# Decoder layer with cross attention: end of the program interleaved, first steps rearranged, cross product in high and low parts

## What is computed

```python
x = layernorm(x + attn(x))      # 4 layers: local and linear attention, then a gelu MLP 256-1024-256
x = layernorm(x + xattn(x, ctx) @ Wout + bout)
x = layernorm(x + gelu(x @ W1c) @ W2c)
# xattn: query i sees only key j with j % n_q == i, n_q = 256, 120 keys
mask = j_idx % n_q == i_idx
sim = where(mask, q @ k.T * scale, -max)
out = softmax(sim) @ v
# W1c, W2c: top 32 of 64 primitives by logits, w = softmax(top values)
W1c = einsum('k,kir,kro->io', w, A[idx], B[idx])
```

## Time and profile before

| what | value |
|---|---|
| median of 3 runs | 1010.5 us (1009.2 to 1010.58) |
| profiled execution | 1011.33 us, span 1009.5 us |
| PE, DVE, ACT, POOL busy | 96%, 67%, 56%, 47% |
| chain that ended last | PE 86%, DVE 5%, SP's queue 2%, issue 2% |
| first two steps | 0 to about 98 us |
| context stage and hand-over | 724 to 782 us |
| compose W1, cross product, compose W2 | to 830, to 845, to 904 us |
| last stage | 904 to 1009.5 us |

### The profile page before, as it was taken

One profiled execution on the slowest core, in us unless ns is written; L12 is line 12 of the kernel. 1 busy time (PEld: TensorE's weight loads), 2 busy tenths in 40 slices (PEclk: granted clock), 3 DMA queues, 4 the chain that ended last, 5 costly groups with the idle time before them and its releaser, 6 DMA issues.

```text
span 1009.5 us, 21836 instructions
## 1 busy us (share of the span) xinstructions
PE 966.8 (96%) x8589; PEld 830.4 (82%) x8589; DVE 681.3 (67%) x1457; ACT 568.0 (56%) x1350; POOL 470.5 (47%) x368
## 2 busy tenths in 40 slices
PE   5869999999999999999999999999999989999997
PEld 4658888888888888888888888888888769998887
DVE  6686768677677868676776768676531886767543
ACT  3666666675856666575766766585623443454210
POOL 3346175456826563774547276551426230007441
PEclk9869999999999999999999999999999999999999
DMA  6030000001110000021000002010155793740001
GB/s 200 6 122 1 2 16 2 1 17 51 36 43 17 2 1 17 4 82 43 17 1 1 18 1 85 1 39 11 38 106 138 158 197 82 163 78 1 21 22 43
DMA packets 71549, 47.57 MB, mean 47 GB/s; under 512 B 44479, under 2 KB 68127, under 8 KB 71455
## 3 DMA queue, kind: packets, MB, share of 16 engines
q1 hardware_dynamic: 71455, 46.27, 18.1%
HBM read 44.16 MB, written 2.10 MB: 46 GB/s over the span
## 4 chain that ended last, share of the span: by engine, by line
PE 86%; DVE 5%; SPq 2%; issue 2%; ACT 2%; POOL 2%; DMA 1%; DVEq 0%; POOLq 0%; ACTq 0%
PE F L1446 19%; PE F L1293 18%; PE A L1293 14%; PE A L1602 4%; PE A L1391 4%; PE A L1749 4%; PE A L1349 3%; PE F L1306 3%; PE A L1408 2%; PE A L1306 2%; PE F L1286 2%; PE A L1722 1%; PE A L1286 1%; PE A L1382 1%; PE A L1365 1%
## 5 line engine op out<-in xcount | busy, mean ns | idle before, releaser
L1293 PE MATMUL F<-xt,w 128*128 128x512 f32 x864 | 218.6, 401 | 4.6 <-ACT scratch L1277 3.9
L431 POOL TENSOR_TENSOR ht<-scratch,ht 128x512 fp32r<-128x512 f32 x128 | 175.6, 1391 | 42.5 <-ACT ht L1081 41.0
L1293 PEld LDWEIGHTS F<-xt,w 128*128 128x128 f32 x864 | 157.5, 188 | 45.9 <-ACT scratch L1277 7.6
L1446 PE MATMUL F<-w,ht 128*128 128x256 f32 x1536 | 190.6, 283 | 2.0 <-POOL ht L431 2.0
L1446 PEld LDWEIGHTS F<-w,ht 128*128 128x128 f32 x1536 | 184.0, 189 | 7.8 <-issue 4.6
L419 POOL TENSOR_TENSOR rstd<-var,minus_half 128x4 f32<-128x4 f32 x32 | 37.6, 1174 | 192.1 <-DVE var L552 191.5
L1078 ACT ACTIVATE scratch<-F,b_now 128x512 f32<-128x512 f32 x128 | 87.5, 684 | 36.3 <-POOL ht L431 18.1
L1293 PE MATMUL A<-wa,xt 128*128 128x512 f32 x372 | 89.9, 397 | 0.0
L1081 ACT ACTIVATE ht<-scratch 128x512 fp32r<-128x512 f32 x128 | 81.0, 632 | 4.1
L1293 PEld LDWEIGHTS A<-wa,xt 128*128 128x128 f32 x372 | 69.3, 189 | 16.0 <-issue 0.2
L426 POOL TENSOR_TENSOR x<-x,vec_f 128x1024 f32<-128x1024 f32 x16 | 37.9, 2368 | 94.2 <-DVE scratch L572 94.2
(11 more groups left out here) (224 smaller groups left out, 2012.1 us busy)
## 6 DMA issues: line engine op xcount, KB each, us to landing
raw_f<-in_L_attn_W_dram SPq DMA_DIRECT2D x8, 1024.0 KB, 5.6
scratch<-in_L_ffn_fc_B_dram SPq DMA_DIRECT2D x32, 256.0 KB, 4.6
scratch<-in_L_ffn_fc_A_dram SPq DMA_DIRECT2D x32, 256.0 KB, 3.9
raw_f<-in_L_ffn_fc_A_dram SPq DMA_DIRECT2D x32, 64.0 KB, 3.9
scratch<-in_x_dram SPq DMA_DIRECT2D x1, 2048.0 KB, 12.4
raw_f<-in_L_ffn_fc_B_dram SPq DMA_DIRECT2D x32, 64.0 KB, 3.5
x<-in_x_dram SPq DMA_DIRECT2D x3, 512.0 KB, 6.7
out_dram<-x SPq DMA_DIRECT2D x3, 512.0 KB, 2.9
```

The source lines that it names most:

```text
L431: pool.tensor_tensor(ht[:, 1, m, :], hf[:, m % 2, :], ht[:, 0, m, :].bitcast(F32), ALU.subtract).then_inc(h_lo, 1)
L1293: last = pe.matmul(out, lhs(a, c), rhs(b, c), start=k == 0, stop=k == len(total) - 1)
L1446: last = pe.matmul(F[:, t % 2, 0:D], ht[:, a, c, P * t:P * t + P], w2[:, b, c, :], start=k == 0, stop=k == len(passes) - 1)
```

## The change

Five parts. (1) GpSimd's order in the first steps: one bias addition ahead of the W1 subtractions, the other behind the first `vec_f` bias, W2's subtractions at the end of the second step; `top_weigh` scales `chosen` (64x32) instead of a block of ones (64x128). (2) VectorE clamps the indices as it writes them, and SyncE's loads skip the runtime range check. (3) The context and `Wv Wout` are split in high and low parts (`ctx_rows`, `wvo_part`), the eight mean rows are one product (`mean_row`, `pick` selects the row), and the cross product runs on FP32R parts. (4) `pairs_lo` splits statistics and scaling in halves, VectorE's loop is written out, and pair 1 is multiplied ahead of the last item's output tiles. (5) In the last stage two gelu chunks and one output tile of the item before alternate, W2's parts are emptied between gelu chunks, and the last item is normalised and stored tile by tile. Scheduling changes that are not in the cut below: a wait of SyncE on `wvo_psum` is gone (the wait behind it covers it), and semaphores have new names.

```diff
+        ctx_rows = [[flat.rearrange("p (b t) -> p b t", b=B) for flat in parts] for parts in (
+            (wa_flat[:, 0:1024], wa_flat[:, 1024:2048]), (wa_flat[:, 2048:3072], wo_flat[:, 0:1024]))]
+        wvo_part = [[ht_odd[:, i, D * c:D * c + D] for c in range(DC)] for i in range(2)]
+        mean_row = [xt[1][:, i, 0, 0:D] for i in range(2)]
+        pick = xt[1][:, 0, 1, 0:P]
...
-                    index[0:1, bass.ds(first, 8)], engines=[mybir.EngineType.SP], min_val=0, max_val=PRIMS - 1)
+                    index[0:1, bass.ds(first, 8)], engines=[mybir.EngineType.SP], min_val=0, max_val=PRIMS - 1,
+                    skip_runtime_bounds_check_because="VectorE holds every index between 0 and PRIMS - 1 as it writes them")
...
+            pool_bias(pool, 0, 0, 0)
             split_lo(pool, w1_pieces(), w1_hi, w1_ready, 0)
-            pool_bias(pool, 0, 0, 0)
-            pool_bias(pool, 0, 1, 1)
...
-                if not out:
-                    split_w2_lo(pool, 0)
...
+                if not out:
+                    pool_bias(pool, 0, 1, 1)
...
+                if not out:
+                    split_w2_lo(pool, 0)
...
                 dve.reciprocal(lsum[:, :], A[0:PRIMS, 0, 0:2]).then_inc(top_step, 1)
-                dve.tensor_copy(index[:, :], A[0:1, 0, 64:64 + 2 * TOPK]).then_inc(index_ready, 1)
+                dve.tensor_scalar(index[:, :], A[0:1, 0, 64:64 + 2 * TOPK], 0.0, float(PRIMS - 1), ALU.max,
...
-                    last = dve.tensor_scalar(lw_wide[:, f, :], ones64[:, :], lw[:, f:f + 1], None, ALU.mult)
+                    last = dve.tensor_scalar(weighted[:, f, :], chosen[:, f, :], lw[:, f:f + 1], None, ALU.mult)
...
-                dve.wait_ge(wvo_psum, 2)
+                for c in range(DC):
+                    dve.wait_ge(cross_hi, c + 1)
+                    lo(dve, wvo_part[1][c], A[:, 4 + c, 0:D], wvo_part[0][c]).then_inc(cross_lo, 1)
                 for c in range(DC):
                     for s in range(2):
-                        dve.wait_ge(ctxt_psum, 2 * c + s + 1)
-                        dve.tensor_copy(ctxt[:, c, 4 * s:4 * s + 4, 0:NKV],
-                                        A[:, 2 * c + s, :].rearrange("p (b t) -> p b t", b=4)[:, :, 0:NKV]).then_inc(ctxt_out, 1)
-                dve.wait_ge(ctxt_out, 4)
-                dve.tensor_reduce(ctx_mean[:, :, :], ctxt[:, :, :, 0:NKV], AX_X, ALU.add).then_inc(ctx_sum, 1)
-                dve.wait_ge(ctx_sum, 1)
+                        rows = A[:, 2 * c + s, :].rearrange("p (b t) -> p b t", b=4)[:, :, 0:NKV]
+                        part = [ctx_rows[i][c][:, 4 * s:4 * s + 4, 0:NKV] for i in range(2)]
+                        dve.wait_ge(cross_hi, 2 + 2 * c + s + 1)
+                        lo(dve, part[1], rows, part[0]).then_inc(cross_lo, 1)
+                        dve.tensor_reduce(ctx_mean[:, c, 4 * s:4 * s + 4], rows, AX_X, ALU.add).then_inc(ctx_sum, 1)
+                dve.wait_ge(ctx_sum, 4)
+                dve.tensor_scalar(ctx_mean[:, :, :], ctx_mean[:, :, :], 1.0 / NKV, None, ALU.mult).then_inc(ctx_sum, 1)
+                dve.wait_ge(ctx_sum, 5)
                 for c in range(DC):
-                    last = dve.tensor_scalar(ctxt[:, c, :, NKV:CB],
-                                             ctx_mean[:, c, :].rearrange("p (b o) -> p b o", o=1).broadcast_to([P, B, CB - NKV]),
-                                             1.0 / NKV, None, ALU.mult)
-                last.then_inc(ctxt_ready, 1)
+                    part = [ctx_rows[i][c][:, :, NKV:CB] for i in range(2)]
+                    dve.wait_ge(cross_hi, 6 + c + 1)
+                    lo(dve, part[1], ctx_mean[:, c, :].rearrange("p (b o) -> p b o", o=1).broadcast_to([P, B, CB - NKV]),
+                       part[0]).then_inc(cross_lo, 1)
...
+            def mean_rows():
+                dve.wait_ge(h_psum, FC * ITEMS * DEPTH)
+                for i in range(2):
+                    dve.memset(mean_row[i].bitcast(F32), 0.0).then_inc(mean_zero, 1)
+            def mean_rows_lo():
+                dve.wait_ge(mean_zero, 2)
+                dve.wait_ge(mean_row_hi, 2)
+                lo(dve, mean_row[1][0:B, :], F[0:B, 0, 0:D], mean_row[0][0:B, :]).then_inc(mean_row_lo, 1)
...
                 pair_lo(f, first, 2)
-                norm_stats(q, p)
+                if f == 0:
+                    dve.wait_ge(t_sum, q + 1)
+                norm_stats(q, p, range(2), False)
                 pair_lo(f, first + 1, 3)
+                norm_stats(q, p, range(2, TILES))
                 norm_var(q, p)
-                for j in range(2, count):
-                    pair_lo(f, first + j, 2 + j)
-                norm_scale(q, p)
+                if count > 2:
+                    pair_lo(f, first + 2, 4)
+                norm_scale(q, p, range(2), False)
+                if count > 3:
+                    pair_lo(f, first + 3, 5)
+                norm_scale(q, p, range(2, TILES))
...
+            mean_rows()
             for t in range(TILES):
                 dve_res2(dve, ITEMS * DEPTH - 1, ITEMS - 1, t)
-            dve.wait_ge(t_sum, ITEMS)
-            with dve.Fori(0, ITEMS - 1) as i:
-                pairs_lo(0, 4 * i + 2, 4, i, i)
-            pairs_lo(0, PAIRS - 2, 2, ITEMS - 1, ITEMS - 1)
+            mean_rows_lo()
+            for q in range(ITEMS):
+                pairs_lo(0, 4 * q + 2, 4 if q < ITEMS - 1 else 2, q, q)
...
+            def f_chunks(p, j):
+                f_h_hi_parts(p, (2 * j,))
+                if p == 0:
+                    composed(*w2_part(j), 4 + j)
+                f_h_hi_parts(p, (2 * j + 1,))
             f_xt_lo_part(0)
-            for k in range(4):
-                composed(*w2_part(k), 4 + k)
             for p in range(ITEMS):
-                f_h_hi_parts(p, range(4))
+                f_chunks(p, 0)
+                if p > 1:
+                    norm_scale(2 * ITEMS + p - 2, p - 2)
+                if p:
+                    f_add(p - 1, 0)
+                f_chunks(p, 1)
+                if p:
+                    f_add(p - 1, 1)
                 if p + 1 < ITEMS:
                     f_xt_lo_part(p + 1)
-                f_h_hi_parts(p, range(4, FC))
+                f_chunks(p, 2)
                 if p:
-                    for t in range(TILES):
-                        f_add(p - 1, t)
+                    f_add(p - 1, 2)
+                f_chunks(p, 3)
+                if p:
+                    dve.wait_ge(f_res, TILES * p - 1)
+                    norm_stats(2 * ITEMS + p - 1, p - 1, range(3), False)
+                    f_add(p - 1, 3)
                     dve.wait_ge(f_res, TILES * p)
-                    norm(2 * ITEMS + p - 1, p - 1)
-            for b in range(2):
-                for t in (2 * b, 2 * b + 1):
-                    f_add(ITEMS - 1, t)
-                dve.wait_ge(f_res, TILES * (ITEMS - 1) + 2 * b + 2)
-                norm(3 * ITEMS - 1 + b, ITEMS - 1, range(2 * b, 2 * b + 2))
+                    norm_stats(2 * ITEMS + p - 1, p - 1, (3,))
+                    norm_var(2 * ITEMS + p - 1, p - 1)
+            norm_scale(3 * ITEMS - 2, ITEMS - 2)
+            for t in range(TILES):
+                f_add(ITEMS - 1, t)
+                dve.wait_ge(f_res, TILES * (ITEMS - 1) + t + 1)
+                norm(3 * ITEMS - 1 + t, ITEMS - 1, range(t, t + 1))
...
-                        act.activation(wvo[:, c, :], A[:, 4 + c, 0:D], ACT.Copy).then_inc(wvo_out, 1)
+                        act.activation(wvo_part[0][c], A[:, 4 + c, 0:D], ACT.Copy)
+                        act.activation(wvo[:, c, :], A[:, 4 + c, 0:D], ACT.Copy).then_inc(cross_hi, 1)
+                    for c in range(DC):
+                        for s in range(2):
+                            act.wait_ge(ctxt_psum, 2 * c + s + 1)
+                            act.activation(ctx_rows[0][c][:, 4 * s:4 * s + 4, 0:NKV],
+                                           A[:, 2 * c + s, :].rearrange("p (b t) -> p b t", b=4)[:, :, 0:NKV],
+                                           ACT.Copy).then_inc(cross_hi, 1)
+                    act.wait_ge(ctx_sum, 5)
+                    for c in range(DC):
+                        act.activation(ctx_rows[0][c][:, :, NKV:CB],
+                                       ctx_mean[:, c, :].rearrange("p (b o) -> p b o", o=1).broadcast_to([P, B, CB - NKV]),
+                                       ACT.Copy).then_inc(cross_hi, 1)
                 act_xt_hi(act, 1, n - 1)
...
             step(DEPTH - 1, 3, nxt=False)
             step(DEPTH - 1, 4, attn=False, nxt=False)
+            act.wait_ge(h_psum, FC * ITEMS * DEPTH)
+            act.activation(pick, ident[:, :], ACT.Copy).then_inc(mean_row_hi, 1)
+            act.wait_ge(mean_zero, 2)
+            act.wait_ge(mean_psum, 1)
+            act.activation(mean_row[0][0:B, :], F[0:B, 0, 0:D], ACT.Copy).then_inc(mean_row_hi, 1)
...
             act.wait_ge(pair_done, 2 * PAIRS)
-            for k in range(4):
-                dst, src = w2_part(k)
```

(44 more changed lines are left out.)

69 lines of the change are left out of this document (38 added, 31 removed).

## The result

The changed kernel takes 998.0 us (median of four, 994.8 to 1000.3) against 1010.5 before: a ratio of 0.9875, 95% interval 0.9849 to 0.9901. Forecast were 998.2 us. The profiled execution is the slowest of the four, 1000.3 us with a span of 998.6; the other spans are 993.1 and twice 996.3.

What follows compares the result with a forecast made beforehand. TensorE, busy 96% of the span, was taken as the bound, so only less TensorE work or idle time counts. Terms -2.0 + 0.1 + 1.0 - 2.0 - 3.9 - 4.7 - 0.85 = -12.3 took 1010.5 to 998.2 us, range 994.8 to 1002.8.

Steps and rivals of the forecast that it cites:

- First steps: First two steps: GpSimd's reordering shortens VectorE's scaled rows but delays the columns product by 1.1; net -2.0 us.
- if the clock comes back sooner: First two steps, outer bound: -4.5 us if a small operation finds a gap at once and the clock recovers sooner.
- Hand-over: At 762 us: waits of 1.9 and 1.2 and a mean product of 0.44 against 1.53 and 0.80 saved; +1.0 us.
- short low clock: Hand-over: the 1.9 us wait at 780 brings TensorE to 1.2 GHz, some 3 us more, 1001.2; chance 0.12.
- W1 loop: Loop composing W1: three stalls shrink by 0.55 each through halved scaling, plus 0.35 from dropped range checks; -2.0 us.
- the step that counts them as 0.35 at the last stall: W1 loop: dropping range checks, at least 1.2 us per eight loads, only removes the last stall's extra 0.35.
- Cross product: Cross product: FP32R matmuls replace FP32, VectorE's additions limit the gain, next turn at 840.8 instead of 844.73; -3.9 us.
- The step on the precision: Cross product: 64 FP32 matmuls at 0.22 against 0.12, 1.8 times, so the trace contradicts the skill's four passes.
- Last stage: Last stage: 6.6 us of waits, less 1.2 left in item 0 and 0.7 for a later start; -4.7 us.
- The step that left item 0 with 1.2 us of waits: Last stage: item 0 has no output tiles to mix in, so about 1.2 us of waits remain.
- the one that counted the table load as nothing: Last stage: one W2 copy instead of four ahead of the first gelu gains nothing, as the first chunk is 0.7 later.
- the second rival: Last stage: VectorE's mixed work delays copies GpSimd awaits, losing 3 us of the 4.7, 1001.2; chance 0.12.

Runs made afterwards that it cites:

- e1: The changed kernel with the last stage in its old order, eight gelu chunks and then four output tiles, and four W2 copies ahead of the first gelu: 1004.9 us.
- e5: The changed kernel with the run-time range checks of the index loads back, VectorE's clamp kept: 999.3 us.
- e6: The changed kernel with VectorE's statistics and scaling whole again in the two compose loops instead of in halves: 999.3 us.

## Why the forecast was right, point by point

The sum was right to 0.2 us, in part by luck: in the profiled pair the first steps gave 1.6 and the W1 loop 1.2 less than forecast, while the last stage and the tail gave 0.6 and 0.45 more; with transfers on time the W1 loop gives 0.6 more too.

- **First steps, -2.0.** At full clock the terms hold: W2's subtractions and the second bias addition moved away -3.3 in the profiles, -2.8 between the medians (forecast -2.8), the bias addition in front +1.1 (2.80 against 1.74 us of wait), so -1.7 to -2.2. What the forecast didn't price is that one order runs at different clocks: the first steps of the changed kernel took 63.6 to 67.2 us in the seven profiles that have them. The profiled pair shows -0.4 for this reason. The bound "if the clock comes back sooner" belonged on both sides.
- **Context stage, +0.1:** +0.4, from the starts of the first pair's multiply (762.06 and 761.55) less the third step's start. VectorE's queue was longer by that: TensorE waits 0.23 and 0.63 for it there, where before it waited 0.33.
- **Hand-over, +1.0:** +1.0, by a wrong route. The mean product took 1.03 us and not 0.44, the second wait 0.18 and not 1.2. The first wait was 1.93 as forecast. The rival "short low clock" came true in two of seven profiles, at 1.1 us rather than 3.
- **W1 loop, -2.0:** -2.6 with transfers on time (`e1`), -0.8 in the profiled execution, where the 256 KB loads took 6.9 us to land in the median against 4.9 before. The split was wrong, by one profile for each part: the range checks are the larger (1.75 for a forecast of 0.35), the halves the smaller (0.55 for 1.65). The checks cost SyncE 2.2 us a group and not 1.2, and the step that counts them as 0.35 at the last stall failed: in `e5` that stall alone comes 1.3 later.
- **Cross product, -3.9:** -4.05. The step on the precision was wrong. The row shows 64 records for the 32 FP32 matmuls of the code, four a bank and not eight (in the order of instructions the mean product stands as x2, in the trace as x4), so one takes 0.44 us against 0.12, 3.7 times. The Trainium skill's four passes ("FP8 and Floating Point Precision", TensorE Precision Notes) agree with the trace, against what the prediction says. Applied to 32 matmuls they give 32 x 0.48 = 15 us, near the 14.08 of the row, not 31. The sum escaped since it rested on VectorE's time at 837.1 and on the price of FP32R, not on the price of an FP32 matmul; the mean product, which rested on the latter, did not.
- **Last stage, -4.7:** -6.1 from the first chunk on, +0.8 for its later start, so -5.3. The step that left item 0 with 1.2 us of waits failed, and with it the one that counted the table load as nothing: with one copy ahead of it the load (900.65 to 901.93) is done before the first chunk, whose gelu starts at 902.65, and the 0.83 us at 908.32 went. Item 0 cost no wait at all. By `e1` and `e6` the late statistics and the copies hide each other: with late statistics four copies cost 0.3, without them (before) 0.83. VectorE as the bound of the stage, the second rival, did not come.
- **Tail, -0.85:** -1.3. From the last addition to the end of the last scaling it is 0.88, as forecast (0.32 each for statistics and scaling, the rest in the small operations); another 0.4 comes behind, with the last store, which the forecast left out.

## What to carry over

A wait of TensorE can cost more than its length where it sits in a sparse stretch: the clock can fall behind it, and differently from one execution to the next, so compare such stretches over several profiles or hold the clock with unused matmuls before pricing an order. Prepare what TensorE needs next ahead of a side result that nobody waits for yet. Count instructions in the code before dividing a row's time by its count.
